# Layer 1 of a two-layer graph network: the one-hot of destinations moves from DVE to ACT, and the edge harmonics are read from PSUM

## The reference, cut to what matters

```python
h = jax.nn.silu(edge_scalars @ (Wfc1 / jnp.sqrt(jnp.float32(FC_IN))))
w = h @ (Wfc2 / jnp.sqrt(jnp.float32(FC_H)))        # w0 64, w1 64, w2 32, w3 32
e0 = f0[edge_src]
e1 = f1[edge_src]
mid0 = w0 * e0 * sh0
mid1 = w3 * jnp.einsum('eum,em->eu', e1, sh1) / jnp.sqrt(3.0)
mid2 = w1[:, :, None] * e0[:, :, None] * sh1[:, None, :]
mid3 = w2[:, :, None] * e1 * sh0[:, :, None]
```

## Time and profile before

| | |
|---|---|
| median of 3 runs | 10095.94 us (10092.63 to 10127.31) |
| profiled execution, span in the trace | 8679.9 us |
| profiled execution, time beside its span | not listed |
| busy in the span | PE 88%, DVE 84%, POOL 69%, PE weight load 66%, ACT 37% |
| mean granted TensorE clock | 0.947 |
| largest group in layer 1 by busy time | the gathers, L1504, 1702.3 us |

### The profile page before, as it was taken

How to read it: one execution, slowest core, us unless ns; L and a number is a source line. 1 busy time by engine, 2 the same in 40 slices (tenths; PEclk the granted TensorE clock), 3 DMA queues, 4 the chain that set the end, 5 groups by cost and what they waited for, 6 DMA issues and landing times. The chain is left out here.

```text
span 8679.9 us, 218293 instructions
## 1 busy us (share of the span) xinstructions
PE 7627.6 (88%) x60373; PEld 5771.5 (66%) x60374; DVE 7274.4 (84%) x17597; ACT 3252.4 (37%) x8375; POOL 6016.9 (69%) x5890
## 2 busy tenths in 40 slices
PE   2599999999999999999999999887968888888888
PEld 1487777877877787877787778776644444444445
DVE  4699999999999999999999999775368888888886
ACT  1244444444444444444444444332222222222223
POOL 0477777777777777777777777651037777777774
PEclk9799999999999999999999999987569999999999
DMA  4344444444444444444444444321012222222222
GB/s 53 78 101 99 102 100 101 102 100 101 101 102 101 101 101 99 102 100 100 100 101 102 101 102 100 77 75 29 11 37 67 67 67 67 67 67 67 67 67 61
DMA packets 616622, 725.52 MB, mean 84 GB/s; under 512 B 284132, under 2 KB 390884, under 8 KB 616573
## 3 DMA queue, kind: packets, MB, share of 16 engines
q0 software_dynamic: 225408, 385.00, 20.4%
q1 hardware_dynamic: 391165, 339.92, 15.3%
HBM read 708.40 MB, written 16.06 MB: 83 GB/s over the span
## 5 line engine op out<-in xcount | busy, mean ns | idle before, releaser
L778 PE MATMUL bank_pair<-w_msg,blocks 128*128 128x160 f32 (+2 forms) x15640 | 2078.7, 288 | 126.8 <-DVE blocks L1030 98.2
L720 POOL DMA_INDIRECT got_src<-src_tab,idx x1564 | 1661.5, 1062 | 659.4 <-POOL idx L714 358.5
L778 PEld LDWEIGHTS bank_pair<-w_msg,blocks 128*128 128x128 f32 x15640 | 1972.7, 192 | 218.5 <-DVE blocks L1030 218.5
L1504 POOL DMA_INDIRECT gotf<-f_tab,idx x1568 | 1702.3, 1086 | 514.2 <-issue 477.4
L720 POOL DMA_INDIRECT got_dst<-dst_tab,idx x1564 | 1486.3, 950 | 528.7 <-issue 503.7
L802 PEld LDWEIGHTS bank_pair<-weights_t,product 128*128 128x128 f32 x12896 | 1498.7, 195 | 309.9 <-issue 295.6
L802 PE MATMUL bank_pair<-weights_t,product 128*128 128x128 f32 x12896 | 1575.5, 281 | 9.5 <-ACT weights_t L932 8.2
L1545 PE MATMUL bank_pair<-val,to_node 128*128 128x385 f32 x3136 | 1247.6, 545 | 5.0 <-DVE val L1659 5.0
L1600 ACT ACTIVATE val<-pre,y_edge 128x160 f32<-128x160 f32 x1568 | 542.8, 417 | 1534.0 <-DVE pre L1640 1531.4
L1545 PEld LDWEIGHTS bank_pair<-val,to_node 128*128 128x128 f32 x3136 | 621.6, 208 | 536.8 <-issue 270.1
L767 PE MATMUL bank_pair<-edge,w_edge 64*128 64x512 f32 x3128 | 884.8, 642 | 9.5 <-DVE blocks L1030 9.5
(11 more groups left out here) (268 smaller groups left out, 11950.3 us busy)
## 6 DMA issues: line engine op xcount, KB each, us to landing
rbf<-in_rbf SPq DMA_DIRECT2D x391, 256.0 KB
dst_bc<-in_dst_rows SPq DMA_DIRECT2D x391, 256.0 KB
y<-in_y SPq DMA_DIRECT2D x391, 128.0 KB
y<-in_y SPq DMA_DIRECT2D x391, 96.0 KB
gotf<-f_tab,idx POOLq DMA_INDIRECT x1568, 2.7
got_src<-src_tab,idx POOLq DMA_INDIRECT x1564
got_dst<-dst_tab,idx POOLq DMA_INDIRECT x1564
rbf<-in_rbf SPq DMA_DIRECT2D x392, 32.0 KB, 1.7
```

The costliest lines, as they stand in the source:

```text
L720: pool.indirect_dma_start(out=buf[slot][:, t, :], out_offset=None, in_=table[:, :], in_offset=bass.IndirectOffsetOnAxis(ap=idx[slot][:, c: ...
L778: return nc.tensor.matmul(to, blocks[rows, k, P * t:P * t + P], w_msg[rows, c0:c1], start=start, stop=stop)
L1504: pool.indirect_dma_start(out=got[k][:, t, :], out_offset=None, in_=f_tab[:, :], in_offset=bass.IndirectOffsetOnAxis(ap=idx[k][:, t:t + 1] ...
```

## The change

Three things. First, the one-hot is no longer made by DVE. `less_slot` holds 1 - (slot + 1) = -slot in place of the slot, and ACT computes, per tile, the absolute value of iota + less_slot, that is the distance of the column from the slot (four instructions of 128 columns, with the column of `less_slot` as bias), waits for its own result, and then one Relu over 512 columns of 1 - distance, which is 1 where the distance is 0 and 0 elsewhere. `to_node` has four buffers instead of two. Second, ACT copies the three harmonics sh1 of a group (12 numbers a partition) into columns 192 to 194 of each tile's 256 in the PSUM bank pair of its weights, once PE has written these. Third, DVE reads them there, so that `along` (L1644) and the product into `val` (L1652) have an operand in PSUM; DVE waits for "y_near" instead of "weight" and no longer for "window_sum" of group g-2 or for `y_edge`. PE waits for "to_node" before a window sum. ACT's order in step g becomes: squash(g+2), by_y0(g), bring_y(g+1), mark_nodes(g+1).

```diff
-                    chain.step(dve.tensor_scalar(slot0[:], slot0[:], 1.0, None, ALU.subtract))
+                    chain.step(dve.tensor_scalar(less_slot[:], less_slot[:], -1.0, 1.0, ALU.mult, ALU.add))
...
-        to_node = [tmp(f"to_node1{i}", [P, TILES, P]) for i in range(2)]
+        to_node = [tmp(f"to_node1{i}", [P, TILES, P]) for i in range(4)]
+        apart = tmp("apart", [P, TILES, P])
...
+        y_near = [w[:, :, 192:195].unsqueeze(3) for w in weights]
...
+                    pe.wait_ge(s["to_node"], g + 1)
                     for t in range(TILES):
-                        last = nc.tensor.matmul(win[k // 2], to_node[k % 2][:, t, :], val[k][:, t, :],
+                        last = nc.tensor.matmul(win[k // 2], to_node[k][:, t, :], val[k][:, t, :],
...
+                def bring_y(i, k):
+                    g = i * 4 + k
+                    act.wait_ge(s[f"y{k}"], i * 16 + 16)
+                    act.wait_ge(s["weight"], g + 1)
+                    nc.scalar.activation(y_near[k % 2].squeeze(3), y_edge[k][:, :, 1:4], ACT.Copy).then_inc(s["y_near"], 1)
+
+                def mark_nodes(i, k):
+                    g = i * 4 + k
+                    if not (isinstance(g, int) and g < 4):
+                        act.wait_ge(s["window_sum"], g - 3)
+                    if not (isinstance(g, int) and g == 0):
+                        act.wait_ge(s["to_node"], g)
+                    for t in range(TILES):
+                        last = nc.scalar.activation(apart[:, t, :], iota_row[:], ACT.Abs, bias=less_slot[:, bass.ds(g * TILES + t, 1)])
+                    last.then_inc(s["apart"], 1)
+                    act.wait_ge(s["apart"], g + 1)
+                    nc.scalar.activation(to_node[k][:], apart[:], ACT.Relu, bias=1.0, scale=-1.0).then_inc(s["to_node"], 1)
...
                     if fixed and g == 0:
                         squash(0, 0)
                         squash(0, 1)
+                        bring_y(0, 0)
+                        mark_nodes(0, 0)
                     if not (fixed and g + 2 >= NG_PAD):
                         squash(i + (k + 2) // 4, (k + 2) % 4)
                     by_y0(i, k)
+                    if not (fixed and g + 1 >= NG_PAD):
+                        bring_y(i + (k + 1) // 4, (k + 1) % 4)
+                        mark_nodes(i + (k + 1) // 4, (k + 1) % 4)
...
-                    early = isinstance(g, int) and g < 2
-                    if not early:
-                        dve.wait_ge(s["window_sum"], g - 1)
-                    dve.tensor_tensor(to_node[k % 2][:], iota_row[:].unsqueeze(1).broadcast_to([P, TILES, P]),
-                                      slot0[:, tile_dst(g, 1)].unsqueeze(2).broadcast_to([P, TILES, P]), ALU.is_equal)
                     w, e, o = weights[k % 2], got[k], pre
-                    dve.wait_ge(s["weight"], g + 1)
+                    dve.wait_ge(s["y_near"], g + 1)
...
-                    dve.wait_ge(s[f"y{k}"], i * 16 + 16)
-                    y = y_edge[k][:, :, 1:4].unsqueeze(3)
+                    y = y_near[k % 2]
```

More of the change, by code:

```diff
@@ L1348, in layer1 @@
         "rbf0", "rbf1", "y0", "y1", "y2", "y3", "got0", "got1", "got2", "got3", "idx0", "idx1", "idx2", "idx3", "raw", "tanh", "hidden", "weight",
-        "by_y0", "first_half", "along", "product", "window_sum", "pair_sum", "merged", "more_masks", "more_sum", "more_added",
+        "by_y0", "to_node", "apart", "y_near", "first_half", "along", "product", "window_sum", "pair_sum", "merged", "more_masks", "more_sum", "more_added",
         "zeroed", "meta", "step", "span", "more_step")}
@@ L1355, in layer1 @@
         val = [tmp(f"val{i}", [P, TILES, SUM1]) for i in range(4)]
-        slot0 = tmp("slot0", [P, NG_PAD * TILES])
+        less_slot = tmp("less_slot", [P, NG_PAD * TILES])
         low = tmp("low", [P, PAIRS])
@@ L1391, in _ @@
                     by_group = "p (g t) -> p g t"
-                    chain.step(dve.tensor_copy(slot0[:].rearrange(by_group, t=TILES), tiles))
+                    chain.step(dve.tensor_copy(less_slot[:].rearrange(by_group, t=TILES), tiles))
                     chain.step(dve.tensor_copy(ring_i[:].rearrange(by_group, t=TILES), tiles))
@@ L1399, in _ @@
                     by_pair = "p (q t) -> p q t"
-                    chain.step(dve.tensor_tensor(slot0[:].rearrange(by_pair, q=PAIRS), slot0[:].rearrange(by_pair, q=PAIRS), low8, ALU.subtract))
-                    chain.step(dve.tensor_scalar(slot0[:], slot0[:], float(P), None, ALU.is_lt))
-                    chain.step(dve.scalar_tensor_tensor(slot0[:], ring[:], 1.0, slot0[:], ALU.add, ALU.mult))
-                    chain.step(dve.tensor_scalar(slot0[:], slot0[:], 1.0, None, ALU.subtract))
+                    chain.step(dve.tensor_tensor(less_slot[:].rearrange(by_pair, q=PAIRS), less_slot[:].rearrange(by_pair, q=PAIRS), low8, ALU.subtract))
+                    chain.step(dve.tensor_scalar(less_slot[:], less_slot[:], float(P), None, ALU.is_lt))
+                    chain.step(dve.scalar_tensor_tensor(less_slot[:], ring[:], 1.0, less_slot[:], ALU.add, ALU.mult))
+                    chain.step(dve.tensor_scalar(less_slot[:], less_slot[:], -1.0, 1.0, ALU.mult, ALU.add))
                     chain.step(dve.tensor_copy(low_i[:], low[:]))
```

## The result

The changed kernel takes 10311.76 us (median of 4 runs, 10299.03 to 10323.36) against 10095.06: ratio 1.0206, 95% interval 1.0189 to 1.0224. Forecast were 9886 us. It is slower by 2 per cent where a gain of 2 per cent was expected.

What follows compares the result with a forecast made beforehand. POOL's gather queue was taken to bound layer 1; shorter gathers cut 5.56 to 5.03 us a group, 0.53 x 392 = 210 us. Span 8680 - 210 = 8470, plus a constant 1416, gave 9886 us, range 9840 to 9990.

Steps and rivals of the forecast that it cites:

- POOL's queue is full, and it alone gives the pace: Layer 1: four gathers of 1.086 us with 0.304 us issue each fill POOL's queue, setting 5.56 us a group.
- the 1416 us: Whole kernel: the excess of the runs' median, 10095.94 us, over the profiled span, unexplained and taken as constant.
- the term for the gathers: POOL in layer 1: gathers shorten from 1.086 to 0.945 us, 0.141 each, 0.56 us a group.
- Two-SBUF-input instructions of DVE hold a gather at its start: Layer 1: about 0.13 us after its start a gather waits for such a running instruction to end; mean price 0.141 us.
- the five gathers of the prediction: Timeline of layer 1: four gathers overlapping two-SBUF-input DVE instructions took 1.00 to 1.57 us; one overlapping a PSUM-reading instruction, 0.94.
- The prediction's step for the short sums: DVE's L1657 and L1650 still hold gathers, up to 0.15 us each; 0.03 us a group taken.
- The gathers set the time, so shorter ones give 0.53 us a group: Layer 1: POOL's pace falls from 5.56 to 5.03 us a group, saving 210 us over 392 groups.
- DVE, ACT and PE hide: Layer 1: DVE at 4.19, ACT at 4.34 and PE at 4.56 us a group stay below POOL's pace.
- Each edit costs what its instruction takes or waits: Layer 1: parts costed by instruction durations and waits; ACT's added 2.6 us a group was counted as hidden.
- The one on the slow side: Rival: ACT changes function tables twice a group, 1283 ns a load, giving 10625 us; chance 0.05 with smaller queue slips.
- The first: Rival: another engine takes part of the gain, leaving 9934 us, or 10018 if PSUM reads slow DVE; chance 0.17.

Runs made afterwards that it cites:

- e1: The kernel before, unchanged, profiled again: 10105.57 us, ratio 0.9997, with a span of 10103.9 us.
- g1: The kernel before with a POOL memset of 256 columns behind each gather: 10132.72 us, ratio 1.0058 to before.
- f3: The changed kernel with a POOL memset of 256 columns behind each gather: 9904.99 us, ratio 0.9795 to before.
- f4: The changed kernel with only two of four gathers per group from the fifth group on: 9081.44 us, ratio 0.8984 to before.
- e5: The kernel before with eight more one-column ACT copies per group, needed by nobody: 9990.22 us, ratio 1.0051 to before.
- g3: The changed kernel with the one-hot made for the first four groups only, without later Abs and Relu: 10182.16 us, ratio 1.0099 to before.
- e7: The kernel before with DVE's one-hot made for the first two groups only and used for all: 9958.08 us, ratio 1.0011 to before.
- e3: The changed kernel with y kept in SBUF, so that only the one-hot moves to ACT: 10199.62 us, ratio 1.008 to before.
- g4: The kernel before with only two of four gathers per group from the fifth group on: 9267.4 us, ratio 0.9198 to before.
- e4: The changed kernel with a POOL memset of one column behind each gather: 9966.87 us, ratio 1.0026 to before.
- g2: The changed kernel with a POOL memset of 128 columns behind each gather: 9828.85 us, ratio 0.975 to before.

## Why the prediction was wrong

By its steps:

- *POOL's queue is full, and it alone gives the pace.* True of the trace it was read from, not of the executions that are timed. In those the pace was 6.96 us and POOL idle for 656.6 us on "product" already before the change (e1). This is the step that failed. It hung on "no row shows what that is. I take it as constant", said of the 1416 us. The sign was on the table: a span 14 per cent short of the run time. 547.5 us of it lay in the very stage of the change. Where the term for the gathers was 0.56 us a group (1086 to 945 ns), the timed executions had 992 to 948 ns to give, 0.18 us a group, and the stops took more than that back: the pace went from 6.96 to 7.45.
- *Two-SBUF-input instructions of DVE hold a gather at its start.* Right in the main. The changed kernel has 948 ns, and g1 against f3 shows 1095 against 955 with the same memsets. But the five gathers of the prediction fit better than the rest: in the whole first trace the rule meets the 389 gathers with L1652 to within 4 ns on average (they take 1288), while the 390 with L1644 take 1141 ns, 0.19 us less than it gives. The prediction's step for the short sums does not fit itself, at most 0.15 us a hit and 0.14 on average; with 948 ns in all it is worth next to nothing. The Trainium skill's sentence that spoke against the holding ("SBUF — State Buffer", Who interferes with whom: only the read half is taken, and descriptor generation needs the write half) is not borne out by the 1095 against 955 ns; that section's sentence on GpSimd reading SBUF agrees with them.
- *The gathers set the time, so shorter ones give 0.53 us a group.* Right as a size, 0.56 us, but only with POOL paced so that the stops don't come (f3 against g1).
- *DVE, ACT and PE hide.* The durations were right. y from PSUM cost nothing (0.545 us for L1664), and ACT got through. f4's 4.33 us a group confirms that they would have hidden below 5.03.
- *Each edit costs what its instruction takes or waits.* Wrong where the stops are: 3136 small ACT instructions whose results nobody uses cost 52 us (e5). The change adds five Abs and Relu and one copy per group on ACT against one instruction less on DVE. From g3 to the whole change is 0.0107 of the ratio, about 108 us, which is what the one-hot on ACT costs on top of y in PSUM; from e7 to e3 it is 0.0069, 70 us. Both are differences of ratios from different hours, each with an interval of 0.001 to 0.0034 either way, and so rough.
- *The rivals.* None was this one. The one on the slow side named another cause (table loads, and there are none). The first named the right row ("POOL now idles on product"), but let it cost part of a gain only.

What takes the place: in the timed executions dense runs of gathers bring the queues of SP, DVE and PE to 0.7 us an instruction until the run has landed. Before, a gather was held by DVE for some of its time and DVE's own groups were longer, 4.06 and 5.49 us where nothing else waits (g4's trace). The change takes both brakes off. Groups then run at 3.67 and 5.05 us, POOL's run is not interrupted, and the stop grows from 6.0 to 8.5 us on average, while POOL afterwards stands idle for 8. That it is the density of the gathers is shown (e4, f3, g2 and f4 thin them out in four measures; e4 comes back to before, the others are below it). How the loss divides is not: a shorter DVE group alone brings stops of 6.1 us and no loss (e7), with ACT's one-hot they are 7.7 us (e3), with undisturbed gathers in its place 8.3 (g3). That half of the loss comes with the added instructions is suggested by g3 and e5, not settled. What the common thing is that runs out (the records, a bus, the queues' fetches) stays open.

## What to carry to other kernels

Compare the span of the trace with the time of the runs before reading anything else; when they are 14 per cent apart, the trace is of another regime, and a stage's bound read from it may not be the bound of the timed one. Taking the brake off an engine that feeds the others is no gain by itself: when faster gathers come in bursts, an idle instruction on POOL, here a memset of 128 columns behind each gather, can be worth more than the change (0.975 instead of 1.0206). And test an engine's pace in both directions, since slowing it is the cheapest experiment of all.

## What was not expected of the hardware

- A gather that has begun while DVE's L1652, with both inputs in SBUF, runs takes longer by what is left of that instruction 0.13 us after the gather's start; freed of such instructions its duration is 940 to 1036 ns throughout the layer, against 942 to 1640 in the first trace.
- In the timed executions, register instructions of SP that take 29 ns took up to 1405 ns in the changed kernel, and the queues of SP, DVE and PE took turns of 0.7 us, while POOL's gathers kept their 0.95 us.
- Eight ACT copies of one column a group, wanted by nobody, cost 0.13 us of time a group (52 us over 392, 27 to 76 by the interval).
- With half the gathers the granted TensorE clock is 1.00 over 500 us of layer 1 and PE 98 per cent busy; with all of them it is 0.79, and PE, which stands still in each stop, is busy 74 per cent.
